# The low half of the differences made by ScalarE and a third adding transfer, with high halves and y_4 in another order

## The chip, the cores and the metric

The kernel runs on one core of one Trainium2 chip. The metric is the device time of one execution in microseconds (us). The engines named here: TensorE (PE, matmuls; PEld are its weight loads), VectorE (DVE), ScalarE (ACT), GpSimd (POOL) and SyncE (SP), which only issues transfers. Transfers (DMAs) run on 16 DMA engines that all queues of the core share: queue q1 carries what SP issues, queue q0 what POOL issues.

## The reference

Two stages follow one another. The first is a gated long convolution, the second a mixture of experts. The change touches only the first:

```python
kv = jnp.einsum('bhil,bhjl->bijhl', k_, v_)        # k_ = v_ = context, head_dim 8
y = jnp.fft.irfft(rfft(kv, n=2*L) * rfft(ssm_kernel, n=2*L))[..., :L]
out = y + kv * D[None, None, None, :, None]
out = jnp.einsum('bijhl,bhil->bjhl', out, q_)      # q = layernorm(x)
x = x + jnp.tanh(g_xattn[0]) * out                 # then layernorm and expert gates
```

There are 64 heads; of each head's 8 x 8 products 36 differ, for 16 batches and L = 1024 positions. All is fp32.

## The kernel before

One loop step is one head `h` (`H` = 64, `steady` unrolls four heads, then loops over pairs, then two more). Positions are cut into 8 tiles of 128. The convolution of a head is a product of Toeplitz blocks with the tiles: output tile `a` sums over source tiles `c <= a`. Every fp32 operand is split in a high half (rounded to fp32r) and a low half (what is left), and every product is three matmuls of 128x128 by 128x288 (`thrice`, L693 to L695): high x high, high x low, low x high. Operands are `kv_hi`, `kv_lo` for the products and `tz_*` (Toeplitz) and `sz_*` (sums of two Toeplitz blocks) for the filter. Output tiles 4 to 7 do not take their four far blocks one by one: `shared(h, u, k)` computes a part from the differences of two pairs of tiles (`diff`, split in `u_hi` and `u_lo`) which one output tile adds and its partner subtracts; this trick saves matmuls. `minus_v` on ScalarE writes the negated copy for the partner.

Each engine runs its own program in the order written; semaphores join them. For one head `h`, while the next head `h+1` is prepared:

- TensorE: `conv(h,0)` to `conv(h,3)`, `gates`, `shared(h,0)`, `conv(h,4)` (output tile 4), `turn_x`, `conv(h,5)` with turnings between its halves, `shared(h,1)`, `conv(h,6)`, `conv(h,7)`. `conv(h,0)` waits for the first half of `kv_lo`, `conv(h,4)` (`n == G`) at its very start for the second half; `shared(h,0)` waits for `u_hi` and `u_lo`. From `conv(h,1)` on, the buffer `psY[n % 2]` must have been copied out by ScalarE.
- ScalarE: `conv_out` copies each output tile (L432); `high` (L409) rounds half of `kv` into `kv_hi`; `minus_high` (L415) writes minus that into `kv_lo`; `high_u` (L423) rounds `diff` into `u_hi`; `keys`, `keys_on` (L387, L392) copy the keys two heads ahead; `squares`, `normal_x`, `queries`, `normal_x1` (L464), `columns`, `gate_parts`.
- GpSimd: `roots(0,h)`, then `add_low(h+1, first half)`, `roots(1,h-1)`, `add_low(h+1, second half)`. `add_low` (L357) issues a transfer from `kv` to `kv_lo` that adds: it turns minus the high half into the low half. `roots` (L347 to L350) are the tiny operations of the layer norms.
- VectorE: `pairs` (products, L641, L644), statistics, `residual` (L624), `multiply` and `add_up` (products with the queries), `differences` (L570), and last in the step `low_u` (L578), `diff - u_hi`.
- SyncE issues, in this order, `kT` two heads ahead, `zT` out, the Toeplitz filter of the next head, `out`, `x`, the summed filter `sz` (once `conv(h,7)` is half done) and `z` out.

Of the kernel before, what the change touches and what calls it, by code (L numbers as in the profile page):

```python
# [7 lines left out]
F32 = mybir.dt.float32  # L8
F32R = mybir.dt.float32r
I32 = mybir.dt.int32  # L10
ALU = mybir.AluOpType
ACT = mybir.ActivationFunctionType
# [90 lines left out]
def gated_conv(nc, x, xT, cT, g_xattn, gate_w, expert_bias, filt_hi, filt_lo, z_d, zT_d, logit_d, out):  # L103
# [12 lines left out]
    B, S, L = x.shape  # L116
    H = S // HD
    NT = L // P
# [27 lines left out]
    def blocks(a):  # L146

        if a < G:
            return [("T", a - c, c) for c in range(a + 1)]
        near = [("T", a - c, c) for c in range(G, a + 1)]  # L150
        if a < G + 2:
            return near + [("S", a + 2 - c, c) for c in (2, 3)]
        return [("S", a - c, c) for c in (0, 1)] + near

    with ExitStack() as ctx:
# [52 lines left out]
        kv_set = m.sem("kv_set")  # L208
        sq_set = m.sem("sq_set")
        hi_set, minus_set, lo_in = m.sem("hi_set"), m.sem("minus_set"), [m.sem(f"lo_in{k}") for k in range(2)]  # L210
        u_set, u_hi_set, u_lo_set = m.sem("u_set"), m.sem("u_hi_set"), m.sem("u_lo_set")
        v_done, v_set = m.sem("v_done"), m.sem("v_set")
        y_done, y_set = m.sem("y_done"), m.sem("y_set")
        told = [m.sem(f"told{k}") for k in range(2)]
# [117 lines left out]
        @block.gpsimd  # L332
        def _(pool):
            identity_steps(nc, pool, ident, made)
            nc.gpsimd.memset(eps[:, :], EPS).then_inc(made, 1)
            nc.gpsimd.memset(minus_half[:, :], -0.5).then_inc(made, 1)
            pool.wait_ge(made, 4)

            def roots(k, h):

                def link(ins, n):
                    ins.then_inc(rooted[k], 1)
                    pool.wait_ge(rooted[k], ROOT * h + n)

                pool.wait_ge(told[k], 3 * h + 3)
                wait(pool, xhat_set if k == 0 else z_set, h)
                link(nc.gpsimd.tensor_tensor(root[k][:, 0:1], mv[k][:, 1:2], eps[:, :], ALU.add), 1)  # L347
                link(nc.gpsimd.tensor_tensor(root[k][:, 0:1], root[k][:, 0:1], minus_half[:, :], ALU.pow), 2)
                pool.sem_inc(passed, 1)
                link(nc.gpsimd.tensor_scalar(root[k][:, 1:2], mv[k][:, 0:1], root[k][:, 0:1], -1.0,  # L350
                                             ALU.mult, ALU.mult), 3)

            def add_low(h, u, half):

                pool.wait_ge(minus_set, 2 * h + half + 1)
                pool.sem_inc(passed, 1)
                nc.gpsimd.dma_start(  # L357
                    kv_lo[u][:, keys_of(half)].rearrange("p t b i -> p (t b i)").rearrange("p (x n) -> p x n", x=2).bitcast(F32),
                    kv[half][:, :, :, :].rearrange("p t b i -> p (t b i)").rearrange("p (x n) -> p x n", x=2),
                    accum_op=ALU.add, max_dma_last_dim=8192).then_inc(lo_in[half], 16)  # L360

            add_low(0, 0, 0)
            add_low(0, 0, 1)

            def step(h, u, ahead, back, back2):
                roots(0, h)
                if ahead:
                    add_low(h + 1, 1 - u, 0)
                if back:
                    roots(1, h - 1)  # L370
                if ahead:
                    add_low(h + 1, 1 - u, 1)

            steady(pool, step)
            roots(1, H - 1)

        @block.scalar
        def _(act):
# [40 lines left out]
            def high_u(h):  # L419

                act.wait_ge(u_set, h + 1)
                wait(act, v_done, 4 * h)
                nc.scalar.activation(u_hi[:, :, :, :].rearrange("p t b i -> p (t b i)"),  # L423
                                     diff[:, :, :, :].rearrange("p t b i -> p (t b i)"),
                                     ACT.Copy).then_inc(u_hi_set, 1)

            def conv_out(h, n):
                a = ORDER[n]
# [59 lines left out]
            high(0, 0, 1)  # L488
            minus_high(0, 0, 1)
            high_u(0)  # L490
            keys(1)
            keys_on(1)

            def step(h, u, ahead, back, back2):
                more = not (isinstance(h, int) and h >= H - 2)
                if ahead:
                    squares(h + 1, 0)
                conv_out(h, 0)
                if back2:
                    columns(h - 2, 0)  # L500
                conv_out(h, 1)
                if ahead:
                    high(h + 1, 1 - u, 0)
                if back2:
                    columns(h - 2, 1)
                conv_out(h, 2)
                if ahead:
                    minus_high(h + 1, 1 - u, 0)
                conv_out(h, 3)
                minus_v(h, 0, 0)  # L510
                minus_v(h, 0, 1)
                if back2:
                    gate_parts(h - 2)
                normal_x(h, u)
                if ahead:
                    squares(h + 1, 1)
                conv_out(h, 4)
                queries(h, u, 0)
                queries(h, u, 1)
                if more:  # L520
                    keys(h + 2)
                conv_out(h, 5)
                minus_v(h, 1, 0)
                minus_v(h, 1, 1)
                if more:
                    keys_on(h + 2)
                if ahead:
                    high(h + 1, 1 - u, 1)
                conv_out(h, 6)
                if ahead:  # L530
                    minus_high(h + 1, 1 - u, 1)
                if back:
                    normal_x1(h - 1)
                if ahead:
                    high_u(h + 1)
                conv_out(h, 7)

            steady(act, step)
# [9 lines left out]
        def _(dve):  # L548
# [17 lines left out]
            def differences(h):  # L566

                dve.wait_ge(kv_set, 2 * h + 1)
                dve.wait_ge(sq_set, 2 * h + 1)
                nc.vector.tensor_tensor(diff[:, :, :, :].rearrange("p t b i -> p (t b i)"),  # L570
                                        kv[0][:, 2:4].rearrange("p t b i -> p (t b i)"),
                                        kv[0][:, 0:2].rearrange("p t b i -> p (t b i)"),
                                        ALU.subtract).then_inc(u_set, 1)

            def low_u(h):

                dve.wait_ge(u_hi_set, h + 1)
                nc.vector.tensor_tensor(u_lo[:, :, :, :].rearrange("p t b i -> p (t b i)"),  # L578
                                        diff[:, :, :, :].rearrange("p t b i -> p (t b i)"),
                                        u_hi[:, :, :, :].rearrange("p t b i -> p (t b i)").bitcast(F32),  # L580
                                        ALU.subtract).then_inc(u_lo_set, 1)

            def multiply(h, u, half):

# [67 lines left out]
            nc.vector.tensor_reduce(pick[:, :], ident[:, :].rearrange("p (j e) -> p e j", e=GQ)[:, 0:E, :], AX.X,  # L652
                                    ALU.add).then_inc(picked, 1)
            differences(0)
            low_u(0)
            dve.wait_ge(gate, 1)
            dve.wait_ge(const, 48)

            def step(h, u, ahead, back, back2):
                if ahead:  # L660
                    pairs(h + 1, 0)
                tell_x(h, u)
                if back:
                    residual(h - 1, 1 - u, 0)
                    multiply(h - 1, 1 - u, 1)
                    add_up(h - 1, 1)
                if ahead:
                    pairs(h + 1, 1)
                if back2:
                    logits(h - 2)  # L670
                if back:
                    residual(h - 1, 1 - u, 1)
                multiply(h, u, 0)
                if ahead:
                    differences(h + 1)
                add_up(h, 0)
                if ahead:
                    low_u(h + 1)

            steady(dve, step)  # L680
            residual(H - 1, 1, 0)
# [7 lines left out]
        def _(pe):  # L689
# [11 lines left out]
            def conv(h, u, n, between=None):  # L701
                a = ORDER[n]
                if n == 0:
                    pe.wait_ge(hi_set, 2 * h + 1)
                    pe.wait_ge(lo_in[0], 16 * h + 16)
                    pe.wait_ge(tz_in[u], 2 * uses(h, u))
                if n == G:
                    pe.wait_ge(hi_set, 2 * h + 2)
                    pe.wait_ge(lo_in[1], 16 * h + 16)
                if a < G:  # L710
                    wait(pe, y_set, NT * h + n - 1)
                terms = blocks(a)
                parts = [terms[:2], terms[2:]] if n == NT - 1 else [terms]
                for part in parts:
                    for half in range(2):
                        acc = psY[n % 2][:, half, 0:NB * PAIRS]
# [2 lines left out]
                        for term in part:  # L719
                            kind, d, c = term  # L720
                            if n == G and kind == "S":
                                pe.wait_ge(sz_in, 32 * h + 32)
                            w_hi, w_lo, first = (tz_hi[u], tz_lo[u], 0) if kind == "T" else (sz_hi, sz_lo, 3)
                            last = thrice(acc, w_hi, w_lo, d - first, half_of(kv_hi[u], NT - 1 - c, half),
                                          half_of(kv_lo[u], NT - 1 - c, half), a < G and term is terms[0],
# [7 lines left out]
            def shared(h, u, k):  # L733

                if k == 0:
                    pe.wait_ge(u_hi_set, h + 1)
                    pe.wait_ge(u_lo_set, h + 1)
                pe.wait_ge(y_set, NT * h + 3 + 2 * k)
                for half in range(2):
                    acc = psY[0][:, half, 0:NB * PAIRS]  # L740
# [1044 lines left out]
```

## Time and profile before

| | us |
|---|---|
| median of 3 runs | 4268.14 |
| lowest, highest | 4264.76, 4273.23 |
| the profiled execution | 4265.89 |
| its span in the profile | 4264.1 |
| convolution stage, 64 heads | until about 1940 of the span |
| experts' stage | the rest |

A row of a group of instructions gives line, engine, operation, output<-inputs, shapes, count, then busy time and mean of one in ns, then the idle time of the engine just before them with what ended it. A timeline row gives start (us from the span's start), duration, engine, line. A row of stretches gives its bounds, its length, the busy time of each engine with instruction counts, the granted clock of TensorE (1.00 is full), the share of the 16 DMA engines that was busy, and GB/s. A head is named by its place in time: the head used below starts at 900.1 and ends at 929.6, where the next one starts.

### The profile page before, as it was taken

What the parts mean: (1) busy time and instruction counts of PE and PEld (TensorE: products, weight loads), DVE (VectorE), ACT (ScalarE), POOL (GpSimd) and SP (SyncE); (2) the same over time, 40 slices, a digit from 0 to 9 for tenths busy, and PEclk for the clock granted to TensorE, in tenths of its full rate; (3) what the DMA queues carried; (4) which work ended last, traced back from release to release, by engine and by line L of the source; (5) the groups of instructions that cost most, each with busy time, mean ns of one, the idle gap of its engine ahead of it and who ended that gap; (6) DMA issues with size and microseconds to landing.
All of it is one profiled execution on the core that took longest, in us unless ns stands there. A gap on an engine that the chain in (4) does not pass through costs nothing.

```text
span 4264.1 us, 71266 instructions
## 1 busy us (share of the span) xinstructions
PE 4125.0 (97%) x25930; PEld 3759.3 (88%) x25930; DVE 2600.3 (61%) x2980; ACT 1890.9 (44%) x2451; POOL 987.7 (23%) x1200
## 2 busy tenths in 40 slices
PE   6999999999999999996899999999999999999998
PEld 6999999999999999995788788888898888988986
DVE  5999999999999999995343432222223323323331
ACT  6787777777778777772111111111112212212120
POOL 1333233332333323230000024540011111211111
PEclk9999999999999999997999999999999999999999
DMA  7888988889888898887223234233433433443332
GB/s 168 223 217 212 222 212 220 217 213 221 213 218 218 212 222 212 220 211 126 87 74 104 87 92 129 75 113 97 119 95 97 114 76 97 95 99 99 83 93 47
DMA packets 280375, 634.14 MB, mean 149 GB/s; under 512 B 45840, under 2 KB 111866, under 8 KB 280246
## 3 DMA queue, kind: packets, MB, share of 16 engines
q1 hardware_dynamic: 218582, 413.89, 33.9%
q0 software_dynamic: 61664, 218.41, 26.6%
q8 instruction: 95, 1.56, 0.2%
q14 instruction: 34, 0.28, 0.0%
HBM read 311.03 MB, written 170.16 MB: 113 GB/s over the span
## 4 chain that ended last, share of the span: by engine, by line
PE 49%; DMA 2%; DVE 1%; issue 1%; ACT 0%; SPq 0%; POOL 0%; DVEq 0%; POOLq 0%; ACTq 0%
PE moe_ps L1654 11%; PE moe_ps L1655 11%; PE moe_ps L1656 11%; PE moe_ps L1672 5%; PE moe_ps L1674 5%; PE moe_ps L1673 5%; PE moe_psT L1643 1%; DMA out<-moe_y,moe_add_i 1%; DMA moe_y<-out 1%; DVE moe_zl L1552 1%; DMA out<-moe_y 0%; ACT moe_zh L1324 0%; DVE moe_hid L1565 0%; DVE moe_y L1579 0%; DMA moe_zin<-zT_d 0%
## 5 line engine op out<-in xcount | busy, mean ns | idle before, releaser
L1654 PE MATMUL moe_ps<-moe_zh,moe_w1h 128*128 128x512 f32 (+2 forms) x2368 | 861.1, 364 | 36.6 <-DVE moe_zl L1552 22.1
L1655 PE MATMUL moe_ps<-moe_zl,moe_w1h 128*128 128x512 f32 (+2 forms) x2368 | 859.0, 363 | 0.0
L1656 PE MATMUL moe_ps<-moe_zh,moe_w1l 128*128 128x512 f32 (+2 forms) x2368 | 856.6, 362 | 0.0
L693 PE MATMUL att_psY<-att_kv_hi,att_tz_hi 128*128 128x288 f32 x2560 | 775.4, 303 | 51.4 <-DMA att_kv_lo<-att_kv 43.6
L695 PE MATMUL att_psY<-att_kv_hi,att_tz_lo 128*128 128x288 f32 x2560 | 755.7, 295 | 0.0
L694 PE MATMUL att_psY<-att_kv_lo,att_tz_hi 128*128 128x288 f32 x2560 | 755.5, 295 | 0.0
L1565 DVE TENSOR_TENSOR moe_hid<-moe_ps,moe_act_s 128x512 f32<-128x512 f32 (+2 forms) x148 | 91.6, 619 | 890.1 <-PE moe_ps L1656 871.4
L693 PEld LDWEIGHTS att_psY<-att_kv_hi,att_tz_hi 128*128 128x128 f32 x2560 | 481.6, 188 | 68.4 <-issue 57.8
L1654 PEld LDWEIGHTS moe_ps<-moe_zh,moe_w1h 128*128 128x128 f32 x2368 | 446.0, 188 | 89.2 <-issue 38.1
L1656 PEld LDWEIGHTS moe_ps<-moe_zh,moe_w1l 128*128 128x128 f32 x2368 | 447.7, 189 | 51.3
L1655 PEld LDWEIGHTS moe_ps<-moe_zl,moe_w1h 128*128 128x128 f32 x2368 | 446.5, 189 | 50.6 <-issue 0.2
L694 PEld LDWEIGHTS att_psY<-att_kv_lo,att_tz_hi 128*128 128x128 f32 x2560 | 482.2, 188 | 0.0
L695 PEld LDWEIGHTS att_psY<-att_kv_hi,att_tz_lo 128*128 128x128 f32 x2560 | 481.5, 188 | 0.0
L1672 PE MATMUL moe_ps<-moe_w2h,moe_hh 128*117 128x512 f32 (+1 forms) x1072 | 429.3, 400 | 9.0 <-DVE moe_y L1579 5.8
L1673 PE MATMUL moe_ps<-moe_w2l,moe_hh 128*117 128x512 f32 (+1 forms) x1072 | 421.0, 393 | 0.0
L1674 PE MATMUL moe_ps<-moe_w2h,moe_hl 128*117 128x512 f32 (+1 forms) x1072 | 420.7, 392 | 0.0
L1336 ACT ACTIVATE moe_act_s<-moe_ps 128x512 f32<-128x512 f32 (+2 forms) x148 | 79.7, 539 | 765.3 <-PE moe_ps L1656 765.3
L1341 ACT ACTIVATE moe_hh<-moe_hid 128x512 fp32r<-128x512 f32 (+2 forms) x148 | 85.1, 575 | 711.3 <-DVE moe_hid L1565 711.3
L347 POOL TENSOR_TENSOR att_root<-att_mv,att_eps 128x1 f32<-128x1 f32 x128 | 150.0, 1172 | 1023.0 <-DVE att_mv L558 1009.4
L432 ACT ACTIVATE att_y<-att_psY 128x576 f32<-128x576 f32 x512 | 332.1, 649 | 118.4 <-PE att_psY L695 112.6
L693 PE MATMUL att_psY<-att_kv_hi,att_sz_hi 128*128 128x288 f32 x1024 | 313.1, 306 | 0.0
L409 ACT ACTIVATE att_kv_hi<-att_kv 128x2304 fp32r<-128x2304 f32 x128 | 271.9, 2124 | 80.5 <-DVE att_kv L644 80.5
(188 smaller groups left out, 7926.9 us busy)
## 6 DMA issues: line engine op xcount, KB each, us to landing
att_kv_lo<-att_kv POOLq DMA_DIRECT2D x128, 1152.0 KB, 12.3
att_kT<-in_cT SPq DMA_DIRECT2D x64, 512.0 KB, 11.6
att_xn<-in_x SPq DMA_DIRECT2D x64, 512.0 KB, 5.8
out<-att_x SPq DMA_DIRECT2D x64, 512.0 KB, 4.0
z_d<-att_z SPq DMA_DIRECT2D x64, 512.0 KB, 9.0
zT_d<-att_zT SPq DMA_DIRECT2D x64, 512.0 KB, 5.3
moe_zin<-zT_d SPq DMA_DIRECT2D x64, 512.0 KB, 4.9
moe_y<-out SPq DMA_DIRECT2D x128, 256.0 KB, 4.3
```

Of the source, the lines that this page charges most:

```text
L347: link(nc.gpsimd.tensor_tensor(root[k][:, 0:1], mv[k][:, 1:2], eps[:, :], ALU.add), 1)
L409: nc.scalar.activation(kv_hi[u][:, keys_of(half)].rearrange("p t b i -> p (t b i)"), kv[half][:, :, :, :].rearrange("p t b i -> p (t b i)" ...
L432: nc.scalar.activation(y[a // G][:, a % G].rearrange("p (c b) i -> p c (b i)", c=2), psY[n % 2][:, :, 0:NB * PAIRS], ACT.Copy).then_inc(y_ ...
L693: nc.tensor.matmul(acc, w_hi[:, cols], x_hi, start=start, stop=False, skip_group_check=True)
L694: nc.tensor.matmul(acc, w_hi[:, cols], x_lo, start=False, stop=False, skip_group_check=True)
L695: return nc.tensor.matmul(acc, w_lo[:, cols], x_hi, start=False, stop=stop, skip_group_check=True)
L1654: nc.tensor.matmul(acc, w1h[:, c, cols], zh[:, c, 0:w], start=(c == 0), stop=False)
L1655: nc.tensor.matmul(acc, w1h[:, c, cols], zl[:, c, 0:w], start=False, stop=False)
L1656: last = nc.tensor.matmul(acc, w1l[:, c, cols], zh[:, c, 0:w], start=False, stop=(c == C - 1))
L1672: nc.tensor.matmul(acc, hh[grp.u][:, f, rows], w2h[:, f, cols], start=(f == 0), stop=False)
L1673: nc.tensor.matmul(acc, hh[grp.u][:, f, rows], w2l[:, f, cols], start=False, stop=False)
L1674: last = nc.tensor.matmul(acc, hl[grp.u][:, f, rows], w2h[:, f, cols], start=False, stop=(f == FC - 1))
```

## The change

`u_lo` is no longer made by VectorE. ScalarE writes minus `u_hi` into `u_lo` (`minus_high_u`), and GpSimd issues a transfer that adds `diff` to it (`add_low_u`), after the two of `kv_lo`. `differences` waits for that transfer of the head before, since it overwrites `diff`. ScalarE rounds the second half of `kv` earlier (before `conv_out(h,5)`, not after it), negates it before `conv_out(h,6)`, not after it, and copies the keys later. TensorE does the two `S` blocks of output tile 4 first and its `T` block, which alone needs the second half of `kv`, last; the wait for that half moves there.

```diff
         if a < G + 2:
-            return near + [("S", a + 2 - c, c) for c in (2, 3)]
+            return [("S", a + 2 - c, c) for c in (2, 3)] + near
...
+            def add_low_u(h):
+
+                pool.wait_ge(u_minus_set, h + 1)
+                pool.sem_inc(passed, 1)
+                nc.gpsimd.dma_start(
+                    u_lo[:, :, :, :].rearrange("p t b i -> p (t b i)").bitcast(F32),
+                    diff[:, :, :, :].rearrange("p t b i -> p (t b i)"),
+                    accum_op=ALU.add, max_dma_last_dim=8192).then_inc(u_lo_in, 16)
...
                 if ahead:
                     add_low(h + 1, 1 - u, 1)
+                    add_low_u(h + 1)
...
+            def minus_high_u(h):
+
+                act.wait_ge(u_hi_set, h + 1)
+                nc.scalar.activation(u_lo[:, :, :, :].rearrange("p t b i -> p (t b i)"),
+                                     u_hi[:, :, :, :].rearrange("p t b i -> p (t b i)").bitcast(F32),
+                                     ACT.Copy, scale=-1.0).then_inc(u_minus_set, 1)
...
                 queries(h, u, 1)
-                if more:
-                    keys(h + 2)
+                if ahead:
+                    high(h + 1, 1 - u, 1)
                 conv_out(h, 5)
                 minus_v(h, 1, 0)
                 minus_v(h, 1, 1)
+                if ahead:
+                    minus_high(h + 1, 1 - u, 1)
+                if more:
+                    keys(h + 2)
+                conv_out(h, 6)
                 if more:
                     keys_on(h + 2)
-                if ahead:
-                    high(h + 1, 1 - u, 1)
-                conv_out(h, 6)
-                if ahead:
-                    minus_high(h + 1, 1 - u, 1)
                 if back:
                     normal_x1(h - 1)
                 if ahead:
                     high_u(h + 1)
+                    minus_high_u(h + 1)
                 conv_out(h, 7)
...
+                wait(dve, u_lo_in, 16 * h)
                 nc.vector.tensor_tensor(diff[:, :, :, :].rearrange("p t b i -> p (t b i)"),
...
-            def low_u(h):
-
-                dve.wait_ge(u_hi_set, h + 1)
-                nc.vector.tensor_tensor(u_lo[:, :, :, :].rearrange("p t b i -> p (t b i)"),
...
                 add_up(h, 0)
-                if ahead:
-                    low_u(h + 1)
...
-                if n == G:
-                    pe.wait_ge(hi_set, 2 * h + 2)
-                    pe.wait_ge(lo_in[1], 16 * h + 16)
...
-                parts = [terms[:2], terms[2:]] if n == NT - 1 else [terms]
+                parts = [terms[:2], terms[2:]] if n in (G, NT - 1) else [terms]
...
+                            if n == G and kind == "T":
+                                pe.wait_ge(hi_set, 2 * h + 2)
+                                pe.wait_ge(lo_in[1], 16 * h + 16)
...
                 if k == 0:
                     pe.wait_ge(u_hi_set, h + 1)
-                    pe.wait_ge(u_lo_set, h + 1)
+                    pe.wait_ge(u_lo_in, 16 * h + 16)
```

The prologue (head 0) has `minus_high_u(0)` and `add_low_u(0)` in the same way.

## Rows read from the trace of the kernel before

**Rows 1.** Busy time in stretches: the convolution's steady middle, and the experts' stage.
```profile
1000.00:1500.00 500.00, 494.94 (x3933) 483.44 (x3933) 484.95 (x489) 393.81 (x506) 158.72 (x133) 1.00 0.89 216
1960.00:4264.00 2304.00, 2236.28 (x10956) 1917.31 (x10956) 750.78 (x1115) 387.63 (x529) 401.79 (x680) 0.99 0.39 96
```

**Rows 2.** Whom TensorE waited for, 0 to 1950: us in total, times, longest.
```profile
PE att_psY L693 <- DMA att_kv_lo<-att_kv: 43.6, 11, 40.0
PE att_psO L758 <- DVE att_oT L614: 10.5, 9, 8.1
PE att_psY L693 <- issue: 4.0, 8, 2.1
```

**Rows 3.** Timeline of TensorE: last matmul of gates, shared's first and last, conv 4's first.
```profile
909.27 0.64 PE L775 MATMUL att_psL<-att_zT,att_gate_s 128*32 128x128 f32 x16
909.84 0.40 PE L693 MATMUL att_psY<-att_u_hi,att_tz_hi 128*128 128x288 f32 x1
...
911.28 0.29 PE L694 MATMUL att_psY<-att_u_lo,att_tz_hi 128*128 128x288 f32 x1
911.41 0.29 PE L695 MATMUL att_psY<-att_u_hi,att_tz_lo 128*128 128x288 f32 x1
911.86 0.39 PE L693 MATMUL att_psY<-att_kv_hi,att_tz_hi 128*128 128x288 f32 x1 [0.16 <-issue]
```

**Rows 4.** Timeline of VectorE across two heads.
```profile
931.20 1.35 DVE L578 TENSOR_TENSOR att_u_lo<-att_diff,att_u_hi 128x1152 fp32r<-128x1152 f32 x1
...
948.53 0.42 DVE L644 TENSOR_TENSOR att_kv<-att_kx 128x256 f32<-128x256 f32 x1
```

**Rows 5.** Timeline of ScalarE at the end of the head, and of the queries of the next.
```profile
924.86 0.65 ACT L432 ACTIVATE att_y<-att_psY 128x576 f32<-128x576 f32 x1 [0.36 <-PE att_psY L695]
925.40 2.12 ACT L415 ACTIVATE att_kv_lo<-att_kv_hi 128x2304 fp32r<-128x2304 f32 x1
927.43 1.23 ACT L464 ACTIVATE att_z<-att_x,att_root 128x1024 f32<-128x1024 f32 x1
928.56 1.15 ACT L423 ACTIVATE att_u_hi<-att_diff 128x1152 fp32r<-128x1152 f32 x1
929.63 0.65 ACT L432 ACTIVATE att_y<-att_psY 128x576 f32<-128x576 f32 x1
...
947.19 0.36 ACT L457 ACTIVATE att_qx<-att_psQ 128x192 f32<-128x192 f32 x1
948.99 1.14 ACT L387 ACTIVATE att_kx<-att_kT 128x1024 f32<-128x1024 f32 x1 [1.43 <-DVE att_kv L644]
...
951.29 0.40 ACT L440 ACTIVATE att_psY<-att_psY 128x288 f32<-128x288 f32 x1 [0.15 <-PE att_psY L695]
951.60 0.62 ACT L392 ACTIVATE att_kx<-att_kT 128x384 f32<-128x384 f32 x1
```

**Rows 6.** Timeline of GpSimd: the end of the second roots, and the second adding transfer.
```profile
925.64 1.50 POOL L350 TENSOR_SCALAR att_root<-att_mv,att_root 128x1 f32<-128x1 f32 x1 [0.21 <-POOL att_root L348]
928.52 1.24 POOL L357 DMA_DIRECT2D att_kv_lo<-att_kv  x1 [1.38 <-ACT att_kv_lo L415]
```

**Rows 7.** Transfers issued from 927 to 930: that adding transfer, us from issue to landing.
```profile
att_kv_lo<-att_kv POOLq DMA_DIRECT2D x1, 1152.0 KB, 11.8
```

**Rows 8.** Queues from 930.5 to 940.5: packets, MB, share of the 16 engines.
```profile
q0 software_dynamic: 272, 1.18, 61.8%
q1 hardware_dynamic: 414, 1.48, 42.4%
```

**Rows 9.** The same from 914.5 to 918.5, where q0 is nearly alone.
```profile
q0 software_dynamic: 179, 0.82, 102.3%
```

**Rows 10.** The same over one whole head, 929.61 to 959.13.
```profile
q1 hardware_dynamic: 1272, 4.01, 46.8%
q0 software_dynamic: 544, 2.36, 40.8%
```

**Rows 11.** Timeline of TensorE in the second head: the one long gap and the matmul before.
```profile
78.42 0.29 PE L695 MATMUL att_psY<-att_u_hi,att_tz_lo 128*128 128x288 f32 x1
80.78 0.37 PE L693 MATMUL att_psY<-att_kv_hi,att_tz_hi 128*128 128x288 f32 x1 [2.07 <-issue]
```

**Rows 12.** Busy time in stretches after that gap.
```profile
82.00:85.00 3.00, 3.00 (x14) 2.99 (x14) 2.79 (x4) 0.38 (x1) 0.00 (x0) 0.50 1.03 192
85.00:88.00 3.00, 3.00 (x26) 3.00 (x25) 0.00 (x0) 1.31 (x4) 0.00 (x0) 0.96 0.09 15
...
80.00:90.00 10.00, 9.22 (x60) 9.23 (x61) 6.28 (x8) 4.34 (x8) 0.00 (x0) 0.83 0.56 105
```

More of the change, by code:

```diff
@@ L210, in gated_conv @@
         hi_set, minus_set, lo_in = m.sem("hi_set"), m.sem("minus_set"), [m.sem(f"lo_in{k}") for k in range(2)]
-        u_set, u_hi_set, u_lo_set = m.sem("u_set"), m.sem("u_hi_set"), m.sem("u_lo_set")
+        u_set, u_hi_set, u_minus_set, u_lo_in = m.sem("u_set"), m.sem("u_hi_set"), m.sem("u_minus_set"), m.sem("u_lo_in")
         v_done, v_set = m.sem("v_done"), m.sem("v_set")
@@ L360, in add_low @@
                     accum_op=ALU.add, max_dma_last_dim=8192).then_inc(lo_in[half], 16)
+            def add_low_u(h):
[5 more added lines that the diff above has]
+                    accum_op=ALU.add, max_dma_last_dim=8192).then_inc(u_lo_in, 16)
             add_low(0, 0, 0)
             add_low(0, 0, 1)
+            add_low_u(0)
             def step(h, u, ahead, back, back2):
@@ L490, in _ @@
             high_u(0)
+            minus_high_u(0)
             keys(1)
@@ L573, in differences @@
                                         ALU.subtract).then_inc(u_set, 1)
-            def low_u(h):
-                dve.wait_ge(u_hi_set, h + 1)
-                nc.vector.tensor_tensor(u_lo[:, :, :, :].rearrange("p t b i -> p (t b i)"),
-                                        diff[:, :, :, :].rearrange("p t b i -> p (t b i)"),
-                                        u_hi[:, :, :, :].rearrange("p t b i -> p (t b i)").bitcast(F32),
-                                        ALU.subtract).then_inc(u_lo_set, 1)
             def multiply(h, u, half):
@@ L654, in _ @@
             differences(0)
-            low_u(0)
             dve.wait_ge(gate, 1)
```

## The prediction, made before the changed kernel ran

> **What bounds the kernel now.** I first read the busy time by stretches. The experts' stage is untouched and leaves no trace of the change, so only the 64 heads count. In their steady middle TensorE is busy 494.9 us of 500 and VectorE 485.0, while the DMA engines are busy 89% of the time and ScalarE 79% [rows 1]. So the convolution runs at TensorE's pace, VectorE is close behind, and the third resource with little room is the one that the change loads further: the transfers. A head takes 29.5 us (it starts at 900.1, the next at 929.6).
>
> Next the waits of TensorE. The second half of `kv_lo` and the prologue make up 43.6 us, but 40.0 of it is one wait at the start, so 3.6 us stay in ten places; `turn_o` has 10.5 less one wait of 8.1 after the last head; 4.0 us more are put down to issue, 2.1 of them in the second head [rows 2]. These add up to about 10 us over 63 heads. A modelled matmul end hides part of a gap, so I look at one: shared's last matmul starts at 911.41 and `conv(h,4)`'s first at 911.86, 0.45 apart where neighbours are 0.13 apart [rows 3]. That is 0.32 us lost in a head. The whole prize is therefore between 10 us (the waits) and 63 x 0.32 = 20 us, with 10 us more if the `turn_o` places go as well: 30 us at most. I take 0.3 us a head.
>
> **VectorE's part.** One subtraction of 1.35 us a head goes [rows 4], and all that follows on VectorE moves up by as much until it meets a wait on another engine. That is worth nothing at once, since TensorE is the bound; it pays only where TensorE waits for VectorE or for what VectorE releases, which the 0.3 us above hold. The products of the second half end at 948.95 now [rows 4], 19.3 after their head's start; without `low_u` they end at about 18.0. The new wait of `differences` for the transfer of the head before costs nothing: that transfer has landed at least ten microseconds earlier, as the bounds below show.
>
> **ScalarE's part.** One more activation a head, of the size of `high_u`, 1.15 us [rows 5]. What matters is whether `conv_out(h,7)`, which frees a buffer for the next head, gets late. I count on from the next head's `minus_v` at 951.69, 22.1 after its start at 929.6 [rows 5], in the new order, each with its duration from these rows less 0.1 of overlap: `minus_high` 2.0 (to 24.1), `keys` 1.05 (25.2), `conv_out(6)` 0.55 (25.7), `keys_on` 0.5 (26.2), `normal_x1` 1.15 (27.4), `high_u` 1.05 (28.5), `minus_high_u` 1.05 (29.5). The last `conv_out` can start when its matmuls are done, at 29.5 (929.63 less 900.1). So the added activation just fits; a slip costs up to 0.5 us. Before `conv_out(h,5)` nothing is lost: the queries end at 17.9 (947.55), the rounding of the second half takes 2.1 to 20.1, and `conv_out(h,5)` has waited behind `keys` until 20.5 so far (948.99 and 1.14) [rows 5]. I cost ScalarE at nothing, with 0.5 us a head in the range.
>
> **y_4 in another order.** The same 18 matmuls; the wait for the second half comes after 12 of them, 12 x 0.13 = 1.6 us later. That takes away the gap of [rows 3] if that half lands no later than now.
>
> **The third transfer.** GpSimd issues it last. It can't before `minus_high_u` is done at 29.5, that is at 929.6 in this head; from the end of a `minus_high` (927.5) to the issue of its transfer pass 1.0 us (928.52), so the new one is issued at about 930.6 [rows 5, 6]. It is needed where `shared` starts, at 9.7 in the next head (909.84 less 900.1) [rows 3], at 939.3. That leaves 8.7 us. Ahead of it in the same queue is the second half of `kv_lo`. Its `minus_high` ends 3.3 us earlier than now, but GpSimd must first finish `roots(1, h-1)`, which end at 927.14 now [rows 6] and at about 926.1 when `residual` comes some 1.0 us sooner. So that issue moves from 928.52 to about 926.8, and with the 11.8 us it needs now [rows 7] it lands at 938.6.
>
> How long does the third one take behind it? While the second half is on its way the engines are full: q0 has 61.8% and q1 42.4% of them, and q0 moves 1.18 MB in 10 us, 118 KB a microsecond [rows 8]. Almost alone q0 moves 0.82 MB in 4 us, 205 KB a microsecond [rows 9]. The third transfer is 128 x 1152 x 4 bytes = 590 KB: 2.9 us alone, 5.0 us beside SP's. It lands between 938.6 + 2.9 = 941.5 and 943.6, so TensorE waits between 2.2 and 4.3 us in every head. I take 3.5, nearer to the shared pace, because SP's Toeplitz loads start at 938, and because the second half itself now runs beside the `sz` loads as well, which so far came before it. The wait doesn't shrink when the head gets longer, since both the transfer and its use are tied to the end of the head before. As a cross-check of the load alone: the DMA engines are busy 87.6% of 29.5 us [rows 10], 25.9 us, and 2.9 more make 28.8. They would fit on average, but not before the date.
>
> **The clock.** The only long gap in the heads now, 78.42 to 80.78 [rows 11], is followed by three microseconds at a granted clock of 0.50 (1.2 GHz), in which 14 matmuls start where the next three have 26 [rows 12]. The ten microseconds from 80 have a clock of 0.83, so that cost 10 x 0.17 = 1.7 us. A gap of 3.5 us is longer than this one, so I add 1.7 us a head.
>
> **The sum.** Per head -0.3 + 3.5 + 1.7 = +4.9 us. Head 1 already has such a gap with its clock, so 62 heads count: 304 us. In head 0 the third transfer is queued behind the second half too, and I put 1 us on it. Together +305. On the profiled execution's 4265.9 that is 4571; the median is 2.2 us above that execution, so 4573, and I say 4572.
>
> **The rivals.**
> (a) The wait is there but the clock mostly holds: then -0.3 + 3.5 = 3.2 us a head, 62 x 3.2 = 198, 4467. For it: the steady middle, with its short gaps, stands at 1.00 [rows 1], and a single gap in the heads shows the fall. Against it: that one had 2.36 us and cost 1.7.
> (b) The wait is short: q0's share grows while SP's queue runs empty. With the lower bound of 2.2 and no fall of the clock, 1.9 us a head, 118 us: 4386.
> (c) The transfer lands in time, and the kernel is faster. Its place is `shared`'s first wait and its price is the prize, 0.3 to 0.5 us a head: 19 to 30 us, 4243. It decides at 939.3: both transfers, 1.77 MB, from about 928.3 have to be in by then, in 10.5 us with half a microsecond for the landing, so q0 needs about 168 KB a microsecond. Alone it has 205, beside SP's queue 118. For it speaks that `kT` and `z` could be done sooner; against it the engines that are full from 930.5 to 940.5, with 104% [rows 8]. The Trainium skill's page "DMA: Bandwidth & Descriptors" has in "Anatomy of one DMA" a fit of 2.0 us plus bytes over 436 GB/s for such a transfer. By that rule the third takes 3.4 us, would be in at 934 and this rival would win; the trace does not agree with it for the transfers it shows, of which one of twice the size takes 11.8 us [rows 7], not 4.7.
> (d) The pieces cancel, the wait being as long as the gaps that go: within 0.2%.
> That the change does nothing isn't open: the subtraction is gone from VectorE and a transfer is there instead.
>
> **Chances.** Forecast 0.53, (a) 0.23, (b) 0.12, (c) 0.08, (d) 0.04. Within 0.2% is about what a measurement can tell from no change. Slower by more: 0.53 + 0.23 + 0.12 = 0.88; faster 0.08; same 0.04. The range reaches from just under (b), 4375, to the upper bound of the wait with clock and ScalarE's slip: (4.3 + 1.7 + 0.5 - 0.3) x 62 = 384, and some for a clock that stays low longer, 4670. Below it lie (c), (d) and a tail of (b).
>
> **What the profile after would show.** Right: a row of TensorE at L693, `u_hi` with `tz_hi`, waiting for the transfer into `u_lo` with 60 entries and over 130 us; a granted clock under 0.98 in 1000 to 1500; the wait for `kv_lo` gone from the steady heads; the third transfer issued about 1 us after the head starts and landing at 12 to 14; VectorE's busy share down from 97% to under 85%; DMA share at or over 0.88 though the head is longer. `conv_out(h,7)` at the end of its matmuls shows the ScalarE count right. Wrong: if u's transfer lands before 9.7 in its head, the step that fails is q0's pace, and the time is that of (c). If there is a long wait and a clock of 1.00, it is (a). If TensorE waits at `conv(h+1,1)` for L432, ScalarE's order was under-counted.

## The result and the profile after

| | before | after |
|---|---|---|
| median, us | 4268.28 (4264.76 to 4273.23) | 4638.39 (4626.12 to 4642.91) |
| ratio after / before | | 1.0862 (95% interval 1.0838 to 1.0885) |
| span of the profiled execution | 4264.1 | 4636.7 |
| mean granted clock of TensorE | 0.99 | 0.959 |

The change makes the kernel 8.6% slower: 370 us on the medians and 372.6 on the profiled spans. Busy time in stretches, in the columns of [rows 1], first the steady middle of the convolution and then the experts' stage:

```profile
1000.00:1500.00 500.00, 437.84 (x3277) 429.26 (x3277) 387.84 (x393) 345.70 (x435) 131.27 (x126) 0.93 0.79 196
2330.00:4636.00 2306.00, 2237.76 (x10954) 1917.34 (x10954) 750.87 (x1114) 387.78 (x529) 405.36 (x670) 0.99 0.39 95
```

The experts' stage has the same work in it and changes little: from its first matmul to the end it is 2289.0 us in this trace and 2281.4 before. Over all runs of this document that stretch varies from 2280.4 to 2293.7, and the cause is open. Some 363 of the 372.6 us arise before `shared` of the last head starts. In the convolution TensorE falls from 494.9 busy us in 500 to 437.8, and what it does run takes longer, at a mean clock of 0.93 where [rows 1] has 1.00. VectorE falls from 485 to 388. Whom TensorE waited for, 0 to 2320, the list of [rows 2]:

```profile
PE att_psY L703 <- DMA att_u_lo<-att_diff: 251.5, 58, 5.5
PE att_psY L703 <- DMA att_kv_lo<-att_kv: 40.4, 1, 40.4
PE att_psY L703 <- issue: 22.2, 6, 5.9
```

The wait for `kv_lo` is back to the one at the start, `turn_o`'s places are gone but for the last, and a new wait of 4.3 us in 58 heads stands above all; the six entries under "issue" are the same wait in the other heads. Together they are 273.7 us in 64 heads. One head begins at 1063.80 and the next at 1100.21. TensorE in it, to be held beside [rows 3]:

```profile
1072.98 0.65 PE L785 MATMUL att_psL<-att_zT,att_gate_s 128*32 128x128 f32 x16
1078.40 0.60 PE L703 MATMUL att_psY<-att_u_hi,att_tz_hi 128*128 128x288 f32 x1 [4.78 <-DMA att_u_lo<-att_diff]
1078.81 0.44 PE L704 MATMUL att_psY<-att_u_lo,att_tz_hi 128*128 128x288 f32 x1
1079.05 0.44 PE L705 MATMUL att_psY<-att_u_hi,att_tz_lo 128*128 128x288 f32 x1
...
1084.16 0.29 PE L704 MATMUL att_psY<-att_kv_lo,att_tz_hi 128*128 128x288 f32 x1
1084.29 0.30 PE L705 MATMUL att_psY<-att_kv_hi,att_tz_lo 128*128 128x288 f32 x1
```

After a gap of 4.78 us the matmuls start 0.24 us apart (1078.81, 1079.05) until about 1083.4, and 0.13 apart after it (1084.16, 1084.29). That is a granted clock of 0.50, the lower of its two levels (1.2 GHz). The next row shows it as a stretch:

```profile
1078.50:1082.00 3.50, 3.50 (x15) 3.50 (x16) 1.79 (x2) 0.71 (x3) 0.00 (x0) 0.50 1.05 278
```

GpSimd's issue of the third transfer, ScalarE's end of the head, and the time from issue to landing of that transfer (shortest, median, longest of 500 to 1500):

```profile
1064.36 0.90 POOL L366 DMA_DIRECT2D att_u_lo<-att_diff  x1 [2.37 <-ACT att_u_lo L441]
```

```profile
1098.81 1.17 ACT L441 ACTIVATE att_u_lo<-att_u_hi 128x1152 fp32r<-128x1152 f32 x1
1100.24 0.65 ACT L450 ACTIVATE att_y<-att_psY 128x576 f32<-128x576 f32 x1 [0.25 <-PE att_psY L705]
```

```profile
DMA to landing us min/median/max: 11.9/13.7/14.2
```

It is issued 0.6 us into the head and lands 13.7 us later (median; 13.8 here), where 9.1 us were left. `conv_out(h,7)` waits for TensorE, not the other way. The queues in the first 14 us of that head, as in [rows 8]:

```profile
q0 software_dynamic: 415, 1.77, 65.4%
q1 hardware_dynamic: 566, 1.87, 38.3%
```

The 1.77 MB are exactly the two adding transfers, and they need the whole stretch: 126 KB a microsecond.

That is one of two kinds of heads, which take turns. In this one `sz` was issued in the same moment as the second half of `kv_lo` (1060.79 and 1060.76), and q0's first packets begin only 3.6 us after that issue. In the next, from 1100.21, the second half was issued 4.7 us ahead of the head's start, its packets began after 1.8 us, and it landed at 1105.7. The third transfer, issued at 1100.58, still took 13.3 us. From 1104.6 to 1106.6, between the two, q0 all but stands still while q1 has the engines:

```profile
q1 hardware_dynamic: 281, 0.73, 95.1%
q0 software_dynamic: 16, 0.00, 0.5%
```

So a shared pace is one part of the lateness. The other part is a late start, of the second half in one head and of the third transfer in the next. TensorE's wait is 4.9 us (mean) in the first kind and 3.7 in the second.

### The profile page after: what moved, and what is told of

Its sections match the earlier page's. It is cut to its first block and busy times, and to the rows that moved or that the text cites. A ratio compares the mean times of both kernels' runs of the same rounds, so it can differ in the third digit from the quotient of the medians.

```text
span 4636.7 us, 71528 instructions
## 1 busy us (share of the span) xinstructions
PE 4232.6 (91%) x25930; PEld 3871.4 (83%) x25930; DVE 2530.2 (55%) x2916; ACT 1970.7 (43%) x2515; POOL 1006.3 (22%) x1264
## 5 line engine op out<-in xcount | busy, mean ns | idle before, releaser
L703 PE MATMUL att_psY<-att_u_hi,att_tz_hi 128*128 128x288 f32 x512 | 190.5, 372 | 273.8 <-DMA att_u_lo<-att_diff 251.5
L703 PEld LDWEIGHTS att_psY<-att_u_hi,att_tz_hi 128*128 128x128 f32 x512 | 123.4, 241 | 290.4 <-issue 290.4
L347 POOL TENSOR_TENSOR att_root<-att_mv,att_eps 128x1 f32<-128x1 f32 x128 | 96.4, 753 | 1144.4 <-DVE att_mv L578 1122.9
## 6 DMA issues: line engine op xcount, KB each, us to landing
att_u_lo<-att_diff POOLq DMA_DIRECT2D x64, 576.0 KB, 13.8
att_kT<-in_cT SPq DMA_DIRECT2D x64, 512.0 KB, 13.7
```

Of the source, the lines that this page charges most:

```text
L703: nc.tensor.matmul(acc, w_hi[:, cols], x_hi, start=start, stop=False, skip_group_check=True)
```

## The experiments

All ratios are to runs of the kernel before on the same chip, whose medians there were 4263.4 to 4265.9 us.

**The orders alone.** The subtraction is back on VectorE; the other edits stay.

```diff
-                    add_low_u(h + 1)
...
-                    minus_high_u(h + 1)
...
                 add_up(h, 0)
+                if ahead:
+                    low_u(h + 1)
```

> Only the new orders are kept (high halves, keys, y_4); the low half of the differences is VectorE's subtraction again and there is no third transfer. Theory (the whole loss is the third transfer's late landing): TensorE's waits in the steady heads nearly vanish and the time is that of before less up to 0.3 us a head, 4245 to 4268. Rival (the new orders cost something of their own, conv_out 7 or 5 being late on ScalarE): 0.5 us a head or more, 4290 to 4300.

Measured: 4271.03, ratio 1.0015 (1.0005 to 1.0025). TensorE's waits, 0 to 2320, without the experts' rows:

```profile
PE att_psY L709 <- DMA att_kv_lo<-att_kv: 40.3, 1, 40.3
PE att_psY L709 <- ACT att_psY L456: 21.1, 57, 0.5
```

The time lies between the two offered ranges. The gap at y_4 is gone, and a wait for `minus_v` has come in its place. ScalarE's rounding of the second half now stands before `conv_out(h,5)`, and with VectorE not relieved its input comes late. So the orders are worth nothing on their own, and they are no part of the 370 us. What they are worth with VectorE relieved, this run can't tell; see the control below.

**The transfer alone.** The orders of the kernel before, with the third transfer.

```diff
-            return [("S", a + 2 - c, c) for c in (2, 3)] + near
+            return near + [("S", a + 2 - c, c) for c in (2, 3)]
...
+                if ahead:
+                    high(h + 1, 1 - u, 1)
                 conv_out(h, 6)
+                if ahead:
+                    minus_high(h + 1, 1 - u, 1)
```

> Only the third transfer and ScalarE's negation are kept; high halves, keys and y_4 stand as before. Theory: the second half of kv_lo is issued some 1.7 us later, so the third transfer, queued behind it, lands 1 to 2 us later than in the changed kernel and each head is longer by as much: 4700 to 4760. Rival (the third transfer's landing depends on its own issue alone): the issue is at about the same place, so within 20 us of the changed kernel's 4638.

Measured: 4758.45 in one run, at the upper end of the expectation. The issue-to-landing time stays as it was (median 13.6 us); what moves is when the transfer can be issued, and TensorE's clock, which is 0.91 in 1000 to 1500 where the changed kernel has 0.93. The orders save 120 us of a loss that the transfer alone brings.

**Less beside it: no sums.**

```diff
                     load_x(h + 1, 1 - u)
-                    load_sums(h + 1)
...
-                                pe.wait_ge(sz_in, 32 * h + 32)
+                                pe.wait_ge(sz_in, 32)
```

> The changed kernel without the loads of the summed filter for heads 1 to 63 (head 0's is used for all), so 2 x 320 KB less on SyncE's queue just as the transfers of kv_lo and u_lo run. Output tiles 4 to 7 then come from the wrong filter. Theory (the DMA engines are full and shared): 2.2 us of engine time go, u_lo lands about 2 us earlier, the gap ahead of shared shrinks from 4.6 to about 2.5 us: 4440 to 4510. Rival (the third transfer is slow by itself, by its issue, its descriptors or its adding): no change, 4638.

Measured: 4649.57 in one run: the rival's number. The queues in the first 14 us of a head:

```profile
q0 software_dynamic: 361, 1.52, 63.0%
q1 hardware_dynamic: 507, 1.80, 38.1%
```

With 655 KB less to load, q1 still moves 1.80 MB in this stretch (1.87 in the changed kernel), and q0's share is as it was. `kT`, `z`, `zT` and the filter simply move up. So taking these bytes out of q1 did not help, as q1 had something left to send through nearly all of the stretch. My reading is that the queues take turns, so that only an empty q1 frees q0; this run does not show that. By this run alone the rival stood equally well, hence the next ones.

**Half the size.**

```diff
-                    u_lo[:, :, :, :].rearrange("p t b i -> p (t b i)").bitcast(F32),
-                    diff[:, :, :, :].rearrange("p t b i -> p (t b i)"),
+                    u_lo[:, 0:1].rearrange("p t b i -> p (t b i)").bitcast(F32),
+                    diff[:, 0:1].rearrange("p t b i -> p (t b i)"),
```

> The changed kernel with the third transfer cut to one of its two tiles, 288 KB instead of 576; the other tile of u_lo keeps minus the high half, so that part of the result is wrong. Theory: at the shared pace of 118 KB a microsecond the transfer is 2.5 us shorter, the gap shrinks to about 2.1 us, and part of the slow clock goes too: 4380 to 4480. Rival (latency of one more queued transfer, whatever its size): over 4600.

Measured: 4550.21 in one run, between the two. The transfer of half the size still takes 12.5 us from issue to landing (median), 1.2 less than the whole. Most of the 13.7 us is therefore not the transfer's own bytes but the time before its turn. Both a slow pace beside q1 and a late start fit that.

**Filling the gap.** The same late transfer, but TensorE is kept at work.

```diff
                 if k == 0:
+                    for _ in range(36):
+                        nc.tensor.matmul(psL[:, L_AT + 16:L_AT + 16 + 240], tz_hi[u][:, 0:P], tz_hi[u][:, 0:240],
+                                         start=True, stop=True, skip_group_check=True)
                     pe.wait_ge(u_hi_set, h + 1)
```

> The changed kernel with 36 matmuls of 240 columns more, between the gates and shared's first wait, into unused columns of a PSUM bank: about 4 us of TensorE work where it stands idle for 4.6. Theory (the gap costs its length and then a slow clock of 1.5 to 2 us a head): the clock stays at 1.00, so that the kernel gets faster by doing more, 4530 to 4580. Rival (the slow clock is no part of the loss, or the transfer is late by TensorE's own pace): 4638 or longer.

Measured: 4534.7 in one run. With 36 matmuls more in each head the kernel is 104 us faster than the changed one:

```profile
1000.00:1500.00 500.00, 495.11 (x3987) 485.54 (x3987) 409.29 (x417) 366.97 (x462) 140.26 (x134) 1.00 0.84 206
```

The clock stays at 1.00. The transfer's issue-to-landing time is the same (median 13.7 us), so what is gained is the price of the clock. 104 us over 63 heads are 1.65 us a head, and that is a little too low: in every second head the added matmuls end 0.5 us after the landing. The part of the head behind the wait has no such flaw. From the start of `shared` to the issue of the next third transfer pass 21.81 us in the changed kernel and 19.95 here (means of 60 heads), so the clock costs 1.86 us a head.

**An emptier q1: SyncE's order** (e7_sp_late, e7 in later quotations). `z` and the keys are issued behind `zT`.

```diff
-                if not (isinstance(h, int) and h >= H - 2):
-                    load_keys(h + 2)
                 if back2:
                     store_zT(h - 2)
+                    store_z(h - 2)
+                if not (isinstance(h, int) and h >= H - 2):
+                    load_keys(h + 2)
...
                     load_sums(h + 1)
-                if back:
-                    store_z(h - 1)
```

> The changed kernel with SyncE's order changed: z and the keys two heads ahead are issued after zT (6 us into the head), not at its start, so that beside the adding transfers only the summed filter is loaded. Theory (the third transfer is late because q0 shares the engines with SP's queue): u_lo lands 3 to 4 us sooner, at about 10 instead of 13.9, the gap falls under 1.5 us and the clock holds: 4270 to 4380. Rival (adding transfers are slow by themselves, or the landing depends on GpSimd's issue): 4600 or more.

Measured: 4296.04, ratio 1.0076 (1.0062 to 1.009): 342 of the 370 us are back, and the transfer is the same, from the same issue. The queues in the first 10 us of a head, and TensorE's wait, 500 to 1500:

```profile
q0 software_dynamic: 414, 1.77, 88.3%
q1 hardware_dynamic: 224, 0.62, 16.5%
```

```profile
PE att_psY L703 <- DMA att_u_lo<-att_diff: 21.5, 17, 2.0
```

The 1.77 MB now go in 10 us and not 14. From 918 to 923, inside that stretch, q1 sends nothing and q0 moves 212 KB a microsecond:

```profile
q0 software_dynamic: 245, 1.06, 105.2%
```

This is the step that the run without sums could not show: the same transfers get 126 KB a microsecond beside a q1 that always has something, and 212 once it is empty. The wait has 17 entries in some 34 heads: every second head, at 1.3 us each.

**A part of it: only the keys later.**

```diff
-                if not (isinstance(h, int) and h >= H - 2):
-                    load_keys(h + 2)
                 if back2:
                     store_zT(h - 2)
+                if not (isinstance(h, int) and h >= H - 2):
+                    load_keys(h + 2)
```

> The changed kernel with only the load of the keys moved behind zT; z stays where it was. Theory (bytes beside q0 between the end of a head and shared make u_lo late): half of what e7 moved, so a gap of 2 to 3.5 us and a clock that falls in part of the heads: 4380 to 4540. Rival (one of the two is the whole cause): 4296 if it is the keys, 4638 if it is z.

Measured: 4487.19 in one run, issue to landing 11.5 us (median). 512 KB moved out of the stretch give 151 us and 2.2 us of landing; the keys and `z` together give 342 and 4.6. So the keys are not the whole cause; `z` alone was not tried.

**The third transfer first.**

```diff
                 if ahead:
-                    add_low(h + 1, 1 - u, 1)
                     add_low_u(h + 1)
+                    add_low(h + 1, 1 - u, 1)
...
+                if ahead:
+                    high_u(h + 1)
+                    minus_high_u(h + 1)
+                conv_out(h, 6)
                 if ahead:
                     minus_high(h + 1, 1 - u, 1)
...
-                if ahead:
-                    high_u(h + 1)
-                    minus_high_u(h + 1)
                 conv_out(h, 7)
...
+                if ahead:
+                    differences(h + 1)
                 multiply(h, u, 0)
-                if ahead:
-                    differences(h + 1)
```

> The changed kernel with the third transfer ahead of the second half of kv_lo: VectorE makes the differences before multiply, ScalarE rounds and negates them right after minus_v and the second half after conv_out 6, GpSimd issues u first. Theory (the landing is set by what lies ahead in q0 and beside it): u_lo lands before the head ends and nobody waits for it; the second half of kv_lo lands at 14 to 16 where y_4's last block needs it at 13.3, a wait of 1 to 3 us: 4330 to 4500. Rival (the wait goes with the number of adding transfers, wherever they stand): the sum of the waits stays at 4.4 us a head, 4600 to 4660.

Measured: 4308.0 in one run, under the expected stretch. u lands 7.3 us after its issue (median) and nobody waits for it. The wait that I expected at y_4 did not come. The waits of TensorE, 0 to 2320:

```profile
PE att_psZ L775 <- ACT att_z L482: 41.6, 62, 4.7
PE att_psY L702 <- DMA att_kv_lo<-att_kv: 40.5, 1, 40.5
```

What is left is ScalarE: `normal_x1` is now late for `turn_z`, 0.6 us in a head. Together with SyncE's later order it is no better:

> The third transfer ahead of the second half of kv_lo and SyncE's later order, together. Theory: both halves land in time, TensorE has no wait left in the steady heads and a clock of 1.00: 4255 to 4285, that is the time of before. Rival (DMA work as a whole has become the bound, 28.8 us of a head and more): 4330 or more.

Measured: 4308.93, ratio 1.0107 (1.0093 to 1.0122), with the same 41.6 us in 62 places. The expectation of 4255 to 4285 left ScalarE out.

**Two tries to clear the rest** (the first is called e10 in the second's text), both on top of SyncE's later order. First the sums behind the second adding transfer, then behind the third.

```diff
                     load_x(h + 1, 1 - u)
+                    sp.wait_ge(u_hi_set, h + 2)
                     load_sums(h + 1)
```

> The kernel of e7_sp_late, and SyncE issues the summed filter only when u_hi is written (28.7 us into the head), so that the second adding transfer is in q0 before it. In e7 every second head had a wait of 1.2 to 1.7 us, where the loads of the summed filter were issued at the same moment as that transfer and its first packet came 3.5 us after its issue, not 1.7. Theory (an adding transfer starts late behind loads already in q1, and late means late for u): all heads become like e7's better ones, 29.26 us instead of 29.64 before: 4235 to 4255, under the time of before. Rival (DMA work as a whole, or the alternation of filter buffers, makes every second head long): 4285 to 4305 as in e7.

Measured: 4322.52, ratio 1.0131 (1.0114 to 1.0148). Both offered numbers missed. The wait for `u_lo` is in 58 heads now (69.6 us): the sums left the quiet end of the head and ran beside q0.

```diff
+                if back:
+                    sp.wait_ge(u_lo_in, 16 * h + 16)
+                    load_sums(h)
                 if back2:
                     store_zT(h - 2)
...
-                    load_sums(h + 1)
```

> The kernel of e7_sp_late with the summed filter of head h loaded only when u_lo of head h has landed (it is needed 2 to 4 us later, by y_4), so that SyncE's queue is empty from the end of one head until u_lo is in. Theory (it is only what runs beside q0 between the end of a head and shared that makes u_lo late; e10 put the sums right into that stretch and made all heads late): the second half of kv_lo lands at about 4.5, u_lo at 7.5 to 8.5, TensorE waits for neither, every head takes 29.3 us, 4235 to 4260. If the sums then land after 11.7, the wait moves to y_4: 4270 to 4300. Rival (adding transfers need 1.77 MB over q0's own pace and a start delay that no order removes): u_lo at 10 or later, 4300 or more.

Measured: 4397.08, ratio 1.0314 (1.0299 to 1.0328). The time missed. It falls where the rival put it, but not by the rival's mechanism: u was to land at 10 us or later, and it lands in time. The queues in the first 8 us of a head, u's time from issue to landing, and TensorE's waits, both 500 to 1500:

```profile
q0 software_dynamic: 344, 1.51, 103.8%
```

```profile
DMA to landing us min/median/max: 6.5/7.6/8.0
```

```profile
PE att_psY L705 <- DMA att_sz_lo<-filt_lo: 52.9, 32, 3.0
```

With nothing on q1, q0 has the engines alone and moves 1.51 MB in 8 us, 189 KB a microsecond. Both kinds of late start are gone as well: the second half's packets begin 1.8 us after its issue in every head, and q0 never pauses between the two. u lands in 7.6 us instead of 13.7, early enough. But then the sums come after it and are late themselves, 1.7 us a head, and this wait too lowers the clock in some heads (0.99 over the middle).

**The control.** SyncE's order on the kernel before.

> The kernel before, with e7's order on SyncE and nothing else. Both theories: TensorE is its bound and waits little, so 4255 to 4270, no more than 0.2% from before. If it is faster by more, what e10 gains would come from SyncE's order and not from the third transfer.

Measured: 4264.91, ratio 0.9998 (0.9988 to 1.0008). That order is worth nothing where there is no third transfer. The trace adds something about the prize. The gap at y_4 is gone here too, since the adding transfers land sooner (median 9.5 us after their issue, 12.4 before), yet the time is the same, because waits for VectorE have come in its place (0 to 1950; [rows 2] has 10.5 in 9 places):

```profile
PE att_psO L758 <- DVE att_oT L614: 18.9, 29, 8.1
```

So VectorE is nearly as much the bound as TensorE, and the gap alone buys nothing. With VectorE relieved, the new orders and SyncE's order all together (e7), the heads in which TensorE doesn't wait for u take 29.3 us from one `shared` to the next, where a head took 29.7 before and takes 29.6 in this control.

No version with the third transfer reached the time of before; the best was 0.8% above it.

## Why the prediction was right, point by point

- **The bound and the prize.** Right: TensorE bound, little to win. The 0.3 us a head that I took stood for the orders and VectorE's relief together. Neither the orders alone (ratio 1.0015) nor an earlier second half alone (0.9998) won anything, but both with the relief won about 0.3 in e7's heads without a wait. My upper bound of 30 us had 10 us for the `turn_o` places, for which [rows 2] has only 2.4.
- **VectorE.** Right in kind: its busy share fell from 97% to 78%, and the kernel is slower all the same, since the wait is for a transfer. Part of the fall is only that heads are longer. That the relief is "worth nothing at once" was too strong: without it the gap at y_4 only changes its place.
- **ScalarE at nothing.** Right: ahead of `conv_out(h,7)` ScalarE is idle for 0.25 us and waits for TensorE, not TensorE for it. The cover was as thin as counted. In the two kernels with u first, where the same activations stand in another order, another one of them, `normal_x1`, comes late and costs 0.6 us a head.
- **The issue.** Counted at 1.0 us into the head, measured 0.6.
- **The landing and the wait.** The step with the size that was off. I put the landing 11.9 to 14.0 us into the head and took a wait of 3.5 us; in one kind of head it lands at 14.5 us and in the other at 13.3 (means), and the wait is 251.5 / 58 = 4.3 us, at the top of my 2.2 to 4.3. Of the two halves of that sum neither held, and that the total came close was partly luck. I had the second half land 9.0 us into the head and the third transfer 2.9 to 5.0 after it. In one kind of head the second half lands at 10.3, as it started late, and the third 4.2 us after it; in the other the second half lands at about 5.5 and the third only 7.7 after it, as it starts late itself. I had no such late starts in the sum. The reason I gave for leaning to the upper end, the sums running beside it, was not it: without them nothing changed. `kT` and `z` keep q1 filled.
- **The clock.** Forecast 1.7 us a head from one gap in the trace, measured 1.65 to 1.9 by the filled gap.
- **The sum.** Forecast +305, measured +370. The waits are 274 us where I had 218, the clock at 1.86 us a head is about 115 where I had 105, and what remains of the 363 us before the last `shared` is a gain of some 26 us, 0.4 a head, where I had 19. So the wait makes 56 us of the miss, the clock 10, and the prize takes 7 off. Of the last 9 us on the profiled spans, 7.6 lie in the experts' stage, where I had put nothing and the cause is open.
- **The signs.** All came as forecast, or within half a microsecond of it, but one: the DMA share was to be at or over 0.88 and is 0.79. My own numbers spoke against that sign, since 28.8 us of transfers in a head of 29.5 + 4.9 us are 0.84.
- **The rivals.** (a), a clock that holds, is what the filled gap shows: 4535, but with a wait of 4.3 us; its own 4467 had 3.5. (b) and (d) are refuted. (c), a transfer in time, is what the emptied q1 shows: it needed about 168 KB a microsecond and has 189 there, against 126 in the changed kernel. The condition was the right one; the profile of before gave the answer in [rows 8]. Its price of 0.3 us a head shows only in e7's heads without a wait; its time, 4243, was reached by no kernel. The Trainium skill's fit on the page "DMA: Bandwidth & Descriptors", section "Anatomy of one DMA", gives 3.4 us for this transfer, by an estimate from its figures. The traces do not agree: with nothing on q1 it took 7.6 us behind the other adding transfer, and 7.3 where it was first in q0 (e8).

## What to carry to other kernels

Before work is moved from an idle-looking resource to the transfers, ask when it must be done and what is then ahead of it in its queue and beside it on the engines. An average DMA share of 0.89 hid a stretch of ten microseconds at 104%, and the deadline lay in it. Here 655 KB less on the other queue did not help as long as it stayed filled, and keeping it empty before the deadline did. A saving that moves one wait can bring up another behind it, as at y_4. And a gap in TensorE can cost more than its length: those of 4.3 us cost 1.9 us more through the clock, which can be measured directly by filling the gap with idle matmuls.

## What the hardware showed that I had not expected

- Taking 655 KB off q1 left q0's time unchanged, and the engines, still at a share of 101%, moved less: 3.32 MB in 14 us against 3.64. Why packets took longer there is open.
- An adding transfer of 288 KB took 12.5 us from issue to landing and one of 576 KB 13.7, behind the same work.
- The heads alternate, in the changed kernel (waits of 4.9 and 3.7 us) and in the one with SyncE's later order, where only every second head had the wait, though all heads do the same. In those heads the sums and the second adding transfer were issued together; I took this for the cause, but separating them (the two last tries) moved the wait and did not remove it. What sets the alternation is open.
- q0 can pause while it has work: in every second head of the changed kernel it does so for 0.2 to 1.9 us (1.6 median) between two adding transfers, the second of which was issued some 4 us before the pause. With q1 empty (e13) it never does. How a filled q1 holds it up is open.
